# Up and gate projection by seven half-sized products from block 2 on

## The chip, the core and the metric

The kernel runs on one core of one Trainium2 chip. The time is that of the device, in microseconds; before the change it is 2041.45 us, the median of three runs (2039.95 to 2041.57). A core has TensorE (PE) for products, VectorE (DVE), ScalarE (ACT), GpSimd (POOL) and SyncE (SP), which here mostly issues transfers.

## The reference

One layer with modulated layer norms on x of 4 x 1024 x 512: attention with 16 heads over one shared key and value head, then a gated network. The change lies in the network, cut here to what matters:

```python
x = fwht(x * SU_ug) / SCALE
x_up = x @ W_up.T * (Wscale_ug[:INTER] * SCALE)        # 512 -> 2048
x_gate = x @ W_gate.T * (Wscale_ug[INTER:] * SCALE)
x = jax.nn.silu(x_gate) * x_up
x = fwht(x * SU_dp) / SCALE
x = x @ W_down.T * (Wscale_dp * SCALE)                 # 2048 -> 512
```

All arrays are float32. The kernel multiplies them as fp32r, each operand split in a rounded part and a rest, so that one product takes three (rounded by rounded, rounded by rest, rest by rounded).

## The kernel before

After the attention the network runs in 8 blocks (numbered 0 to 7) of 512 tokens. A block has 16 steps (`FT`), numbered f from 0, one for every 128 of the 2048 inner features; g = 16 x block + f counts 128 steps. In step g PE makes up and gate of these 128 features for the block's 512 tokens (`up_gate`: 2 x 4 key tiles x 3 = 24 products of 512 columns), then adds the previous step's share to the four output tiles (`down(g - 1)`: 12 products), so that the other engines have one step to turn up and gate into y.

- SyncE loads the raw weights of step g + 3 (`upgate_raw`, 512 KB, a ring of three) and the down weights of step g + 2 (`d_ring`, 512 KB), both from DRAM, in program order with everything else on its queue.
- ScalarE rounds the raw weights of step g + 1 into `w_ring` (`cast_upgate`), VectorE makes their rest (`split_upgate`).
- When up and gate are done, ScalarE makes silu of the gate, VectorE multiplies it with up and the scale (`weighted`), casts y and makes its rest. `y_mul` counts the product, `y_ready` the split; PE's down products wait for `y_ready`, and `up_gate(g)` for `y_mul` of step g - 2.

Around it each block prepares the next: SyncE loads its rows (`x_in`, `load_block`) in step 1, after the previous block's outputs are stored; VectorE makes the layer-norm statistics in step 2 (`block_statistics`) and the normed rows in step 4; PE transposes them in steps 6 and 7 (`turn`); VectorE combines the four key tiles in steps 8 and 9 (`cross`); in step 10 these are split, and in steps 11 and 12 PE multiplies them with a Hadamard matrix (`had_tile`) into the next block's input `h_t_split`. Step 0 of a block also holds `outputs` of the block before: four output tiles times their gain, and four residual additions, all on VectorE. Block 0 carries the last projection tiles of the attention as well (`TAIL_TILES`).

Every engine works through its own instructions in the order written; semaphores join them. GpSimd does nothing in the network. Nothing plans the order: it is that of the loops and step numbers.

Of the kernel before, what the change touches and what calls it, by code (L numbers as in the profile page):

```python
# [10 lines left out]
P = 128  # L11
D = 512
# [92 lines left out]

def side_work(H, heads):
# [69 lines left out]
def program(nc, io, B, S):  # L176
# [8 lines left out]
    dram = dict(x1=x1_dram, gains=gains_dram, inverse=inverse_dram, qw=qw_dram, across=across_dram, down=down_dram)  # L185
    ctx = ExitStack()
    with ctx:
# [61 lines left out]
        phase(nc, io, dram, B, S, sem, banks, K, A, W, Z, F)  # L249
# [35 lines left out]
def phase(nc, io, dram, B, S, sem, banks, K, A, W, Z, F):  # L285
# [5 lines left out]
    across_rows, down_rows = dram["across"], dram["down"]  # L291
# [14 lines left out]
    ugr, wr, dr, sg, y, ys, gbw, out_sb = (F[n] for n in ("ugr", "wr", "dr", "sg", "y", "ys", "gbw", "out_sb"))  # L306
    up_bank, gate_bank, acc = banks[:, 0:2, :], banks[:, 2:4, :], banks[:, 4:8, :]
# [49 lines left out]

    places = side_places(B)
# [5 lines left out]
    def free_bank(g, k):  # L364

        return banks[:, (g + 1) % 2 + 2 * (k % 2), :]

# [15 lines left out]
    with nc.Block() as block:  # L383

        @block.sync
        def _(sp):
# [93 lines left out]
            def network(g):  # L480
                blk, f = divmod(g, FT)
                if g + UG_RING < STEPS:
                    load_upgate(g + UG_RING)
                if 2 <= g + 2 < STEPS and g:
                    load_down(g + 2)
                if f == X_STEP:
# [120 lines left out]
        def _(act):  # L607
# [89 lines left out]

            def deviations(nb):
# [17 lines left out]
            def network(g):  # L716
                blk, f = divmod(g, FT)
                nb, ahead = blk + 1, blk + 1 < BLOCKS
                if g + 1 < STEPS:
                    cast_upgate(g + 1)  # L720
                act.wait_ge(ug_done, g + 1)
# [4 lines left out]
                if ahead and f == DEV_STEP:  # L726
                    deviations(nb)
                if ahead and f in TURN_STEPS:
                    for k in TURN_STEPS[f]:
                        act.wait_ge(turned, (nb - 1) * KT + k + 1)  # L730
                        turn(nb, k, free_bank(g, k)).then_inc(h2_ready, 1)
                if ahead and f == HI_STEP:
                    round_crossed(nb, range(KT))
                if ahead and f in HAD_STEPS:
                    for k in HAD_STEPS[f]:
# [902 lines left out]
```

## Time and profile before

| | us |
|---|---|
| median of 3 runs | 2041.45 |
| lowest, highest | 2039.95, 2041.57 |
| the profiled execution | 2041.26 |
| its span, first to last instruction | 2039.5 |
| PE busy in it | 1973.9 |
| DVE busy | 1184.8 |
| ACT busy | 794.3 |
| POOL busy | 162.6 |

The busy time of PE counts matmuls whose ends are modelled, so 97% says only that PE is seldom without one. The profile is of one execution; 1.8 us lie around its span.

### The profile page before, as it was taken

What the parts mean: (1) busy time and instruction counts of PE and PEld (TensorE: products, weight loads), DVE (VectorE), ACT (ScalarE), POOL (GpSimd) and SP (SyncE); (2) the same over time, 40 slices, a digit from 0 to 9 for tenths busy, and PEclk for the clock granted to TensorE, in tenths of its full rate; (3) what the DMA queues carried; (4) which work ended last, traced back from release to release, by engine and by line L of the source; (5) the groups of instructions that cost most, each with busy time, mean ns of one, the idle gap of its engine ahead of it and who ended that gap; (6) DMA issues with size and microseconds to landing.
All of it is one profiled execution on the core that took longest, in us unless ns stands there. A gap on an engine that the chain in (4) does not pass through costs nothing.

```text
span 2039.5 us, 26390 instructions
## 1 busy us (share of the span) xinstructions
PE 1973.9 (97%) x9120; PEld 1463.3 (72%) x9120; DVE 1184.8 (58%) x2596; ACT 794.3 (39%) x1333; POOL 162.6 (8%) x530
## 2 busy tenths in 40 slices
PE   6899999999999999999999999999999999999998
PEld 3566666666666556556888888888888888888887
DVE  6777676777667655675455455444554455445433
ACT  3366565556555554465221322222222223232121
POOL 3111121112111111121000000000000000000000
PEclk8899999999999999999999999999999999999999
DMA  7433443334342555635335334344343353443431
GB/s 236 123 98 75 105 114 103 98 84 120 97 115 69 145 160 171 206 118 191 134 134 196 124 127 166 125 132 164 124 165 124 124 171 120 157 141 125 153 125 62
DMA packets 113695, 271.43 MB, mean 133 GB/s; under 512 B 27790, under 2 KB 33166, under 8 KB 113436
## 3 DMA queue, kind: packets, MB, share of 16 engines
q1 hardware_dynamic: 104204, 248.71, 39.9%
q10 hardware_dynamic: 9360, 21.04, 3.1%
q8 instruction: 74, 1.21, 0.3%
q14 instruction: 57, 0.47, 0.1%
HBM read 194.96 MB, written 31.74 MB: 111 GB/s over the span
## 4 chain that ended last, share of the span: by engine, by line
PE 54%; DMA 1%; DVE 1%; POOL 0%; SPq 0%; ACT 0%; issue 0%; POOLq 0%; ACTq 0%; DVEq 0%
PE banks L1311 34%; PE banks L1466 17%; PE banks L1534 1%; PE banks L1402 1%; PE banks L1408 1%; DMA upgate_raw<-in_w_ug 0%; POOL probs L878 0%; PE banks L1511 0%; PE banks L1365 0%; PE banks L1396 0%; DMA inverse_sums_dram<-sums 0%; DVE out_sb L1072 0%; DVE out_sb L1063 0%; DMA o_group<-o_raw 0%; ACT probs L789 0%
## 5 line engine op out<-in xcount | busy, mean ns | idle before, releaser
L1311 PE MATMUL banks<-h_t_split,w_ring 128*128 128x512 f32 x3072 | 717.4, 389 | 1.0 <-DVE w_ring L1037 1.0
L1311 PEld LDWEIGHTS banks<-h_t_split,w_ring 128*128 128x128 f32 x3072 | 576.6, 188 | 121.0 <-DVE w_ring L1037 1.4
L722 ACT ACTIVATE silu_gate<-banks,scale_upgate 128x512 f32<-128x512 f32 x128 | 88.3, 689 | 800.8 <-PE banks L1311 800.8
L1466 PE MATMUL banks<-d_ring,y_split 128*128 128x512 f32 x1536 | 370.5, 390 | 0.1
L1045 DVE SCALAR_TENSOR_TENSOR y<-banks,scale_upgate,silu_gate 128x512 f32<-128x512 f32 x128 | 95.9, 749 | 433.3 <-ACT silu_gate L722 433.3
L789 ACT ACTIVATE probs<-banks 128x512 f32<-128x512 f32 x576 | 312.6, 601 | 60.4 <-PE banks L1511 55.0
L1466 PEld LDWEIGHTS banks<-d_ring,y_split 128*128 128x128 f32 x1536 | 287.3, 188 | 59.5 <-DVE y_split L1051 0.5
L1534 PE MATMUL banks<-probs,v_ones 128*64 128x512 f32 (+3 forms) x1536 | 281.5, 502 | 3.0 <-POOL probs L878 3.0
L1365 PE MATMUL banks<-k_stack,q_stacks 96*128 96x512 f32 (+3 forms) x768 | 252.2, 372 | 16.4 <-ACT neg_max_rows L643 5.7
L1511 PE MATMUL banks<-q_stacks,k_stack 98*128 98x512 f32 (+3 forms) x768 | 251.0, 369 | 6.0 <-ACT probs L789 4.1
L1534 PEld LDWEIGHTS banks<-probs,v_ones 128*64 128x64 f32 x1536 | 119.4, 138 | 164.2 <-issue 136.7
L878 POOL TENSOR_SCALAR_AFFINE_SELECT probs<-probs 128x128 f32<-128x128 f32 x512 | 147.2, 311 | 748.5 <-ACT probs L789 748.5
L1365 PEld LDWEIGHTS banks<-k_stack,q_stacks 96*128 96x128 f32 x768 | 141.7, 192 | 71.8 <-DVE max_all L899 14.9
L899 DVE CUSTOM_DVE_ANT_0 masked_scores<-banks,mask_row,max_all 128x512 f32<-128x512 f32 (+3 forms) x256 | 132.0, 547 | 85.7 <-PE banks L1365 85.1
L1511 PEld LDWEIGHTS banks<-q_stacks,k_stack 98*128 98x128 f32 x768 | 141.3, 191 | 51.5 <-issue 32.7
L902 DVE TENSOR_REDUCE max_all<-banks 128x1 f32<-128x512 f32 x256 | 166.5, 686 | 19.0 <-PE banks L1365 18.7
L1037 DVE TENSOR_TENSOR w_ring<-upgate_raw,w_ring 128x1024 fp32r<-128x1024 f32 x128 | 156.0, 1219 | 17.9 <-ACT w_ring L714 17.6
L767 ACT ACTIVATE o_raw<-banks 128x512 f32<-128x512 f32 x128 | 76.5, 598 | 190.1 <-PE banks L1534 190.1
L899 DVE CUSTOM_DVE_ANT_0 masked_scores<-banks,mask_row 128x512 f32<-128x512 f32 (+3 forms) x256 | 120.0, 486 | 40.1 <-PE banks L1365 38.8
L714 ACT ACTIVATE w_ring<-upgate_raw 128x1024 fp32r<-128x1024 f32 x128 | 135.0, 1055 | 9.5 <-DMA upgate_raw<-in_w_ug 9.5
L1311 PE MATMUL banks<-h_t_split,qw_group 128*128 128x512 f32 x384 | 94.5, 402 | 2.9 <-DVE h_t_split L929 2.5
L1311 PE MATMUL banks<-ow_split,o_split 128*128 128x512 f32 x384 | 93.3, 392 | 2.6 <-DVE q_split L920 2.6
(132 smaller groups left out, 1247.6 us busy)
## 6 DMA issues: line engine op xcount, KB each, us to landing
upgate_raw<-in_w_ug SPq DMA_DIRECT2D x128, 512.0 KB, 4.2
d_ring<-down_split_dram SPq DMA_DIRECT2D x128, 512.0 KB, 3.3
q_stacks<-q_split SPq DMA_DIRECT2D x192, 128.0 KB, 2.5
o_group<-o_raw SPq DMA_DIRECT2D x128, 128.0 KB, 2.3
x<-in_x SPq DMA_DIRECT2D x32, 256.0 KB, 3.0
o_group<-inverse_sums_dram SPq DMA_DIRECT2D x64, 128.0 KB, 2.7
x_and_residual<-in_x SPq DMA_DIRECT2D x32, 256.0 KB, 4.4
x_dram<-x_and_residual SPq DMA_DIRECT2D x32, 256.0 KB, 2.5
```

Source lines behind the costliest of these rows:

```text
L714: nc.scalar.activation(wr[g % 2][:, 0], ugr[g % UG_RING][:], ACT.Copy).then_inc(ug_cast, 1)
L789: nc.scalar.activation(pr[:, u, :], score_bank[:, at % SLOTS_SCORE, :], ACT.Exp, scale=SCALE).then_inc(exped, 1)
L878: last = nc.gpsimd.affine_select(out=triangle, in_=triangle, compare_op=ALU.is_ge, fill=0.0, base=0, pattern=[[1, P]], channel_multiplier=-1)
L899: last = nc.vector.tensor_tensor_reduce(out=masked_scores[:, i % 2, col:col + w], in0=part, in1=mask[:, HALF - w:HALF], scale=1.0, scalar= ...
L902: last = nc.vector.tensor_reduce(out, part, AX.X, ALU.max)
L1037: nc.vector.tensor_tensor(wr[g % 2][:, 1], ugr[g % UG_RING][:], wr[g % 2][:, 0].bitcast(F32), ALU.subtract).then_inc(ug_ready, 1)
L1045: nc.vector.scalar_tensor_tensor(out=y[:], in0=up_bank[:, s, :], scalar=sug[:, 0, f:f + 1], in1=sg[:, s, :], op0=ALU.mult, op1=ALU.mult).t ...
L1311: ins = nc.tensor.matmul(out, weights(a, k), moving(m, k), start=(k == 0 and a + m == 0), stop=(last and k == kts - 1 and a == 1))
L1365: last = nc.tensor.matmul(side[:, r, col:col + w], qst[0:96, s, qt * P:(qt + 1) * P], kst[0:96, b % 2, k0:k0 + w], start=True, stop=True)
L1466: last = nc.tensor.matmul(acc[:, t, :], ys[s][:, a, t * P:(t + 1) * P], dr[g % D_RING][:, m, :], start=(f == 0 and a + m == 0), stop=(f == ...
L1511: last = nc.tensor.matmul(score_bank[:, at % SLOTS_SCORE, col:col + w], kst[0:98, b % 2, kt * P:(kt + 1) * P], qst[0:98, s, q0:q0 + w], st ...
L1534: last = nc.tensor.matmul(obank[half * 2 * HD:(half + 1) * 2 * HD, c, q0 - c * HALF:q0 - c * HALF + w], vs[:, b % 2, kt, :], pr[:, u, col: ...
```

## The change

From block 2 on (`PLAIN = 2`, `FIRST_HALVES = 32`) up and gate are taken as one product of a 2 x 2 block matrix: rows up and gate (128 features each), columns the first and the second 256 keys, times an input of two halves of keys by two halves of 256 tokens (`TOKENS`). Strassen's scheme, in Winograd's form, makes it of seven half-sized products (`ITEMS`) in place of eight: 7 x 2 key tiles x 3 = 42 products of 256 columns.

- Weight items. Three of the seven are weights as they are, four are sums. In block 1 GpSimd makes the sums (`sum_weights`), one set in each step, from the raw weights that lie in `upgate_raw` anyhow; ScalarE rounds them and VectorE or GpSimd makes their rests; ScalarE issues the store of the split set (1792 KB) to `upgate_items_dram`. In blocks 2 to 7 SyncE loads one such set in each step, three steps ahead, into a ring of three (`load_items`); raw weights are no longer loaded, cast and split there.
- Input items. Four of the seven inputs are sums too: GpSimd makes them once a block from a copy of the Hadamard tiles (`sum_inputs`), ScalarE rounds all seven and VectorE makes the rests, in steps 13 to 15.
- Outputs. VectorE adds the seven results up into gate and up (`add_both`, `add_gates`, `add_ups`, `multiply_second`), in halves of 256 tokens. The last of the seven (`UP_LAST`) is multiplied after `down(g - 1)`. ScalarE rounds y now.
- The residual additions move from step 0 to step 1 of a block (from block 2 on).

The diff, cut to its core:

```diff
@@ SyncE
             def load_upgate(g):
                 if g >= UG_RING:
                     sp.wait_ge(ug_ready, g - UG_RING + 1)
+                if g - UG_RING >= FIRST_HALVES - FT:
+                    sp.wait_ge(items_lo, g - UG_RING - (FIRST_HALVES - FT) + 1)
+                    sp.wait_ge(weights_summed, 3 * (g - UG_RING - (FIRST_HALVES - FT) + 1))
                 sp.dma_start(ugr[g % UG_RING][:], io["w_ug"][g % FT]).then_inc(ug_in[g % UG_RING], 16)
+            def load_items(n):
+                if n == 0:
+                    sp.wait_ge(items_out[0], 16 * FT // 2)
+                if n == 1:
+                    sp.wait_ge(items_out[1], 16 * FT // 2)
+                    sp.wait_ge(ug_done, FIRST_HALVES)
+                if n >= HALVES_RING:
+                    sp.wait_ge(products_made, ITEMS * (n - HALVES_RING + 1))
+                r = (n + 2) % HALVES_RING
+                sp.dma_start(wq[r][:].bitcast(F32), items_dram[n % FT]).then_inc(items_in[r], 16)
@@ ScalarE
             def network(g):
+                f, made = g % FT, g - (FIRST_HALVES - FT)
+                if g + 1 < FIRST_HALVES:
                     cast_upgate(g + 1)
+                if made >= 0:
+                    store_items(made)
+                if -1 <= made < FT - 1:
+                    round_items(made + 1)
+                    round_sums(made + 1)
                 act.wait_ge(ug_done, g + 1)
@@ GpSimd
+            def sum_weights(f):
...
+                nc.gpsimd.tensor_tensor(s1, a21, a22, ALU.add).then_inc(weights_summed, 1)
+                nc.gpsimd.tensor_tensor(s3, a11, a21, ALU.subtract)
+                pool.wait_ge(weights_summed, 3 * f + 1)
+                nc.gpsimd.tensor_tensor(s2, s1, a11, ALU.subtract).then_inc(weights_summed, 1)
+                pool.wait_ge(weights_summed, 3 * f + 2)
+                nc.gpsimd.tensor_tensor(s4, a12, s2, ALU.subtract).then_inc(weights_summed, 1)
+                pool.wait_ge(sums_hi, f + 1)
+                nc.gpsimd.tensor_tensor(cw[f % 2][:, 1, 3:ITEMS, :], sraw[:], cw[f % 2][:, 0, 3:ITEMS, :].bitcast(F32), ALU.subtract).then_inc(sums_lo, 1)
@@ VectorE
+            def halves(g):
+                blk, f = divmod(g, FT)
+                if g > FIRST_HALVES:
+                    multiply_second(g - 1)
+                add_both(g)
+                if g > FIRST_HALVES:
+                    split_half(g - 1, 1)
+                add_gates(g)
+                add_ups(g)
+                multiply_first(g)
+                split_half(g, 0)
+                if f == 0:
+                    outputs(blk - 1)
+                if f == 1:
+                    for t in range(NT):
+                        residual(blk - 1, t)
+                if blk + 1 < BLOCKS:
+                    around(g)
@@ TensorE
+            def half_product(g, item):
+                blk, r = g // FT, (g - FIRST_HALVES + 2) % HALVES_RING
+                for k in range(2):
+                    for a, m in ((0, 0), (0, 1), (1, 0)):
+                        last = nc.tensor.matmul(item_bank(g, item), wq[r][:, a, item, k * P:(k + 1) * P], by_key(item_input(blk, item, m))[:, k, :],
+                                                start=(k == a + m == 0), stop=(k == a == 1))
+                last.then_inc(products_made, 1)
...
+            for g in range(FIRST_HALVES, STEPS):
+                half_products(g)
+                for i in range(2):
+                    beside_halves(g, i)
+                    down(g - 1, i * NT // 2, (i + 1) * NT // 2)
+                beside_read(g)
+                last_half_product(g)
             down(STEPS - 1)
```

On VectorE, a plain step of the network before, of 128 features by 512 tokens:

```order
L1037 TENSOR_TENSOR w_ring<-upgate_raw,w_ring 128x1024
L1045 SCALAR_TENSOR_TENSOR y<-banks,scale_upgate,silu_gate 128x512
L1050 CAST y_split<-y 128x512
L1051 TENSOR_TENSOR y_split<-y,y_split 128x512
```

And the same step in block 1 of the changed kernel, where `items_made` and `items_ring` take the weight items:

```order
L1244 TENSOR_TENSOR w_ring<-upgate_raw,w_ring 128x1024
L1273 TENSOR_TENSOR items_made<-upgate_raw,items_made 128x512
L1274 TENSOR_TENSOR items_made<-upgate_raw,items_made 128x256
L1252 SCALAR_TENSOR_TENSOR y<-banks,scale_upgate,silu_gate 128x512
L1257 CAST y_split<-y 128x512
L1258 TENSOR_TENSOR y_split<-y,y_split 128x512
```

Two subtractions stand ahead of the product y. GpSimd, idle before in the network, has these five beside them in the same step (the set after each other one goes to `items_ring`):

```order
L1062 TENSOR_TENSOR weight_sums<-upgate_raw 128x256
L1063 TENSOR_TENSOR weight_sums<-upgate_raw 128x256
L1065 TENSOR_TENSOR weight_sums<-weight_sums,upgate_raw 128x256
L1067 TENSOR_TENSOR weight_sums<-upgate_raw,weight_sums 128x256
L1069 TENSOR_TENSOR items_made<-weight_sums,items_made 128x1024
```

On VectorE again, steps 1 and 2 of a later block of the changed kernel, with what each waits for:

```order
L1304 SCALAR_TENSOR_TENSOR y<-y,scale_upgate,silu_gate 128x256 [waits silu_ready,halves_added]
L1324 TENSOR_TENSOR y_split<-y,y_split 128x256 [waits halves_hi]
L1385 TENSOR_TENSOR out_sb<-out_sb,x_in 128x512 [waits acc_read] x4
L1317 TENSOR_TENSOR y<-y,banks 128x256 [waits halves_added,products_made]
L1304 SCALAR_TENSOR_TENSOR y<-y,scale_upgate,silu_gate 128x256 [waits dve_step]
L1281 TENSOR_TENSOR both<-banks,up_first 128x256 [waits p1_copied,products_made]
L1324 TENSOR_TENSOR y_split<-y,y_split 128x256 [waits halves_hi]
L1288 TENSOR_TENSOR all_gate<-banks,both 128x256 [waits halves_added,products_made]
L1290 TENSOR_TENSOR silu_gate<-banks,all_gate 128x512 [waits y_mul,dve_step]
L1297 TENSOR_TENSOR y<-banks,both 128x256 [waits y_ready]
L1299 TENSOR_TENSOR y<-banks,up_first 128x256 [waits products_made]
```

The residual additions (L1385) now stand at the end of step 1, behind its second split; before, they stood in step 0 right behind the outputs. On SyncE's queue the place of the block load before and after:

```order
L463 DMA upgate_raw<-in_w_ug 128x1024 [waits ug_ready]
L472 DMA d_ring<-down_split_dram 128x1024 [waits d_done]
L478 DMA out<-out_sb 128x512 [waits out_ready] x4
L458 DMA x_in<-x_dram 128x4x512 [waits out_ready]
```

```order
L556 DMA d_ring<-down_split_dram 128x1024 [waits d_done]
L547 DMA items_ring<-upgate_items_dram 128x3584 [waits products_made]
L562 DMA out<-out_sb 128x512 [waits out_ready] x4
L528 DMA x_in<-x_dram 128x4x512 [waits out_ready]
```

The stores and the block load have kept their place in the queue, and what stands ahead of them is an items load of 3584 elements a partition, released by the last product of step 1, where there was one of 1024.

## Rows read from the trace of the kernel before

**Rows 1.** The page, parts 1, 2 and 5: engines, clock by slices, costliest groups.
```profile
PE 1973.9 (97%) x9120; PEld 1463.3 (72%) x9120; DVE 1184.8 (58%) x2596; ACT 794.3 (39%) x1333; POOL 162.6 (8%) x530
...
PEclk8899999999999999999999999999999999999999
...
L1311 PEld LDWEIGHTS banks<-h_t_split,w_ring 128*128 128x128 f32 x3072 | 576.6, 188 | 121.0 <-DVE w_ring L1037 1.4
```

**Rows 2.** The page, part 4: the chain that ended last, shares by line.
```profile
PE banks L1311 34%; PE banks L1466 17%; PE banks L1534 1%; PE banks L1402 1%; PE banks L1408 1%; DMA upgate_raw<-in_w_ug 0%; POOL probs L878 0%; PE banks L1511 0%; PE banks L1365 0%; PE banks L1396 0%; DMA inverse_sums_dram<-sums 0%; DVE out_sb L1072 0%; DVE out_sb L1063 0%; DMA o_group<-o_raw 0%; ACT probs L789 0%
```

**Rows 3.** Busy time by window: one step, and its columns.
```profile
core 0: us, PE busy (x) PEld busy (x) DVE busy (x) ACT busy (x) POOL busy (x), PEclk, DMA share, GB/s
1500.00:1508.16 8.16, 8.16 (x37) 6.76 (x37) 4.56 (x8) 1.64 (x2) 0.00 (x0) 1.00 0.40 124
```

**Rows 4.** The chain in order of time: start us, us, what. Two block starts.
```profile
1597.91 5.45 PE banks L1311 x24
...
1732.14 5.45 PE banks L1311 x24
```

**Rows 5.** Timeline of PE in the attention: start us, us, instructions.
```profile
801.23 0.40 PE L1511 MATMUL banks<-q_stacks,k_stack 98*128 98x256 f32 x2
801.47 2.92 PE L1311 MATMUL banks<-ow_split,o_split 128*128 128x512 f32 x12
```

**Rows 6.** Timelines of GpSimd and VectorE at the start of the program.
```profile
22.99 1.26 POOL L866 TENSOR_TENSOR qw_group<-x_and_residual,qw_group 128x512 fp32r<-128x512 f32 x1 [9.92 <-ACT qw_group L831]
23.01 1.79 DVE L929 TENSOR_TENSOR h_t_split<-kv,h_t_split 128x512 fp32r<-128x512 f32 x1
24.21 1.72 POOL L868 TENSOR_TENSOR kvw_split<-masked_scores,kvw_split 128x512 fp32r<-128x512 f32 x1
...
36.01 1.34 DVE L935 CAST k_stack<-kv 96x512 fp32r<-96x512 f32 x1 [1.78 <-ACT kv L626]
37.39 1.66 DVE L936 TENSOR_TENSOR k_stack<-kv,k_stack 32x512 fp32r<-32x512 f32 x1
```

**Rows 7.** Groups by line, shapes apart: busy us, mean ns | idle before.
```profile
L1037 DVE TENSOR_TENSOR w_ring<-upgate_raw,w_ring 128x1024 fp32r<-128x1024 f32 x128 | 156.0, 1219 | 17.9 <-ACT w_ring L714 17.6
L714 ACT ACTIVATE w_ring<-upgate_raw 128x1024 fp32r<-128x1024 f32 x128 | 135.0, 1055 | 9.5 <-DMA upgate_raw<-in_w_ug 9.5
L1045 DVE SCALAR_TENSOR_TENSOR y<-banks,scale_upgate,silu_gate 128x512 f32<-128x512 f32 x128 | 95.9, 749 | 433.3 <-ACT silu_gate L722 433.3
L1051 DVE TENSOR_TENSOR y_split<-y,y_split 128x512 fp32r<-128x512 f32 x128 | 88.6, 692 | 4.4
L1050 DVE CAST y_split<-y 128x512 fp32r<-128x512 f32 x128 | 54.6, 427 | 4.4
L899 DVE CUSTOM_DVE_ANT_0 masked_scores<-banks,mask_row 128x256 f32<-128x256 f32 x64 | 26.9, 420 | 0.0
L630 ACT ACTIVATE v_ones<-banks 128x256 f32<-128x256 f32 x4 | 1.5, 372 | 0.0
```

**Rows 8.** Timeline of VectorE and SyncE's queue around a block load; its landing.
```profile
1507.78 2.49 DVE L1072 TENSOR_TENSOR out_sb<-out_sb,x_in 128x512 f32<-128x512 f32 x4
1508.49 2.14 SPq L478 DMA_DIRECT2D out<-out_sb  x4
...
1510.67 0.46 SPq L458 DMA_DIRECT2D x_in<-x_dram  x1
...
DMA to landing us min/median/max: 5.9/5.9/5.9
...
1521.71 2.46 DVE L995 BATCH_NORM_STATS2 ln_stats<-x_in 128x6 f32<-128x512 f32 x4
1524.21 0.38 DVE L999 BATCH_NORM_AGGREGATE ln_mean_var<-ln_stats 128x2 f32<-128x6 f32 x4
```

**Rows 9.** Busy time by window: the queue when it is full (columns as above).
```profile
1509.00:1519.00 10.00, 10.00 (x46) 8.29 (x45) 5.41 (x8) 1.64 (x2) 0.00 (x0) 1.00 0.98 351
1514.00:1518.00 4.00, 4.00 (x20) 3.30 (x19) 0.76 (x1) 0.00 (x0) 0.00 (x0) 1.00 1.04 417
```

More of the change, by code:

```diff
@@ new lines, in around, with round_half @@
+            def around(g):
+                blk, f = divmod(g, FT)
+                nb, ahead = blk + 1, blk + 1 < BLOCKS
+                if ahead and f == DEV_STEP:
+                    deviations(nb)
+                if ahead and f == HI_STEP:
+                    round_crossed(nb, range(KT))
+                if ahead and nb >= PLAIN and f in INPUT_STEPS:
+                    round_inputs(nb, INPUT_STEPS[f])
+            def round_half(g, half):
+                n, at = g - FIRST_HALVES, slice(half * TOKENS, (half + 1) * TOKENS)
+                if half:
+                    act.wait_ge(y_mul, g + 1)
+                else:
+                    act.wait_ge(halves_added, ADDED * n + FIRST_MULTIPLIED)
+                    act.wait_ge(d_done, g - 1)
+                nc.scalar.activation(ys[g % 2][:, 0, at], y[:, at], ACT.Copy).then_inc(halves_hi, 1)
@@ L725, in network @@
                         round_group(ALL // 4 - 2 + g // 2, half)
[L726 to L735, printed above, removed]
-                        act.wait_ge(had_done, (nb - 1) * KT + k + 1)
-                        round_had(nb, k, free_bank(g, k))
+                for i in range(2):
+                    read_tile(g, i)
+                around(g)
             def side_step(keys):
@@ L1051, in weighted, with rest_of_inputs @@
                 nc.vector.tensor_tensor(ys[s][:, 1, :], y[:], ys[s][:, 0, :].bitcast(F32), ALU.subtract).then_inc(y_ready, 1)
+            def rest_of_inputs(nb, f):
+                m = nb - PLAIN
+                done = sum(len(INPUT_STEPS[step]) for step in INPUT_STEPS if step < f)
+                for i, item in enumerate(INPUT_STEPS[f]):
+                    dve.wait_ge(inputs_hi, ITEMS * m + done + i + 1)
+                    nc.vector.tensor_tensor(by_key(item_input(nb, item, 1)), input_half(item), by_key(item_input(nb, item, 0)).bitcast(F32),
+                                            ALU.subtract).then_inc(inputs_lo, 1)
@@ new lines, in around @@
+            def around(g):
+                blk, f = divmod(g, FT)
+                nb = blk + 1
+                if f == STATS_STEP:
+                    for t in range(NT):
+                        block_statistics(nb, t)
+                if f == NORM_STEP:
+                    block_inverses(nb)
+                    for t in range(NT):
+                        block_rows(nb, t)
+                if f in (CROSS_STEP, CROSS_STEP + 1):
+                    cross(nb, f - CROSS_STEP)
+                if f == HI_STEP:
+                    for ks in ((0, 1), (2, 3)):
+                        crossed_rest(nb, ks)
+                if nb >= PLAIN and f in INPUT_STEPS:
+                    rest_of_inputs(nb, f)
@@ L1587, in _ @@
             weigh(ALL - 1, 1)
-            for g in range(STEPS):
+            for g in range(FIRST_HALVES):
                 up_gate(g)
```

291 lines of the change are left out of this document (253 added, 38 removed).

## The prediction

> **What bounds the kernel now.** I read the page's busy shares and clock first: TensorE is busy 97% of 2039.5 us, at full granted clock in every slice but the first two [rows 1]. The chain of what ended last says the same by line: 34% products of up and gate, 17% down products, nearly nothing else in the last 800 us [rows 2]. One step of the network is 8.16 us, in which PE never rests while VectorE works 4.56 and ScalarE 1.64 [rows 3]. Of it 24 products of 512 columns take 5.44 us (5.45 in [rows 4]), or 0.2267 each, and the 12 down products the other 2.72. A whole block of 16 steps is 134.2 us (two block starts, 134.23 apart [rows 4]): 130.6 for 16 steps and 3.7 for the transposes and Hadamard tiles. So PE's own work is the price of a block, and anything that makes PE wait is added in full.
>
> **What is removed: columns.** From block 2 on (blocks are numbered 0 to 7), 96 steps issue 42 products of 256 columns instead of 24 of 512: 10752 columns for 12288. The trace has no such row on a 128-row weight, so I bound it. Half of 0.2267 is 0.1133. Two score products of 256 columns, each with its own weights, take 0.24 us from start to next start, 0.12 each [rows 5]. I take 0.117, nearer the row than the rule of three. 42 x 0.117 = 4.91 us against 5.44, 0.53 a step, 96 steps: **-50.5 us** (-65 with 0.1133, -38 with 0.12). A step is then 7.64 us. The recorded 188 ns of a weight load [rows 1] is no spacing: in [rows 5] two loads and two products fit in 0.24 us.
>
> **What is added in block 1: a port that two engines share.** In steps 15 to 31 GpSimd now makes the weight sums: per step four adds of 256 columns and one subtraction of 1024. A subtraction of 512 columns took it 1.26 us [rows 6], so I take, by size, 4 x 0.65 + 2.6 = 5.2 us. VectorE gets two more subtractions (512 and 256 columns). Alone, GpSimd's 5.2 and the 1.05 us in which it waits for ScalarE to round the sums fit in 8.16 us. But [rows 6] show that the two engines exclude each other: a VectorE subtraction from SBUF, 0.69 us for its like [rows 7], took 1.79 beside GpSimd's, and ended 0.55 after it; GpSimd's next took 1.72; a VectorE cast took 1.34 for 0.43 and the subtraction behind it 1.66 for 0.68. The SBUF — State Buffer page of the Trainium skill (Who interferes with whom) has this rule: VectorE with two SBUF inputs, or in a two-port mode, takes a port pair that it shares with GpSimd, and the later one waits for the whole instruction; one PSUM input does not contend. By that rule, and the trace agrees with 1.79 against 0.69, both lists below must be added up; without it this block would cost nothing.
> VectorE's list per step, durations from [rows 7]: the ring split 1.22, the new 0.69 and 0.42, the cast of y 0.43, its rest 0.69, together 3.45. With GpSimd's 5.2 that is 8.65 us a step for one pair, 138.4 in 16 steps. Around them in that block come the rows of the norm (four, at the cast's 0.43) 1.7, the four crossings of 1024 columns 4.9, their rest 2.4, residuals 2.5 [rows 8], seven input remainders 4.8, and GpSimd's four input sums 5.0: 21.3. Together 159.7 us for a block of 134.2. The delay reaches PE because ScalarE's silu stands behind its rounding of the sums, SyncE's next raw load behind both, and the stored items must be back before step 32: **+26 us**. From both sides: 0 if the pair is not the limit, +35 if it also idles half a microsecond a step while GpSimd waits for ScalarE.
>
> **What is moved: the residual, and with it the load of the next block.** Before, outputs and residuals both run in step 0 of a block; the load is issued at 1510.67, right behind them, lands 5.9 us later, and the statistics start only at 1521.71, 5 us after the landing [rows 8]. After, the residuals stand in step 1 behind the second split. Take T2, the start of step 2. SyncE's items load for a later step, 1.835 MB where a raw load was 0.524, is released by step 1's last product and issued at T2 + 0.5. Each residual ends 0.62 after the one before, the last at T2 + 2.4; four stores and the block load are out by T2 + 3.2. That is 1.84 + 1.05 + 1.05 = 3.93 MB in one queue, at 417 GB/s [rows 9] 9.4 us from T2 + 1.4; landing T2 + 11.5. VectorE wants it at T2 + 7.7. It waits, spends 2.9 on the statistics [rows 8], then 0.43 + 0.48 to finish y, and 0.43 on the first sum of step 3, which PE needs before its sixth item: ready at about T2 + 16. PE is there at 5 x 0.70 = 3.5 us into step 3, which began at T2 + 7.7: some 4.7 us of wait. Four blocks give 19, block 2 (its queue still full of items that were stored late) about 7.8: **+26.5 us**. The last block loads nothing. The wait shrinks by 1 us for each microsecond that the load lands earlier, to nothing at T2 + 7.
>
> **Smaller terms.** The last input remainders: VectorE ends its own step at 7.2 and then has two more of 0.69, so the next block starts at 8.5, not 7.64: 0.9 in five blocks and 2 at step 32, **+6.5**. The Hadamard steps wait for ScalarE's copy between two tiles: 0.6 in five blocks, **+3**. At the end the second half of y is added, multiplied, rounded and split only after the last product, 0.43 + 0.48 + 0.37 + 0.43 and the hops, 2.1 us of which 0.5 was waited for before: **+1.6**.
>
> **What lies hidden.** The VectorE work of a steady step: seven of 256 columns (0.42 each, the row of the scores' own 256), two scaled products at 0.48, one of 512, 4.6 us; its chain from the fifth item (3.5 + 0.2) is 0.42 + 0.69 + 0.42 + 0.42 + 0.48, ScalarE's 0.37, and 0.42, done at 7.2 of 7.64 us with hops. So the cover is only 0.45 us; each 0.1 us beyond it would cost 10 us. The transfers: 2.36 MB a step, 309 GB/s, where one queue held 351 over 10 us with gaps and 417 without [rows 9]. In block 1, 1.84 out and 1.05 in make 354 GB/s, near that; it fits, barely.
>
> **Sum.** -50.5 + 26 + 26.5 + 6.5 + 3 + 1.6 = +13. The profiled execution took 2041.26 us (span 2039.5 and 1.8 around it), 0.2 under the median of 2041.45, so the forecast is 2055 us.
>
> **Rivals.** (A) The forecast, 0.46; its own range is 2045 to 2070.
> (B) The shared pair costs little, because GpSimd has half a step of lead and VectorE's idle 3.6 us a step [rows 3] take it up. Then -13: 2029, faster. For it: the sum is 6% over what a step has. Against: the 21.3 us around, and each wait is for a whole instruction. It decides if block 1 takes under 147 us. 0.19.
> (C) The block load is not late, because the queue's transfers interleave: -13.5, 2028. Against: x_in took 5.9 us with only the end of the stores ahead [rows 8]. 0.07.
> (D) Narrow products cost 0.1133 or less: 2055 - 15 = 2040, same or a bit faster; 0.12.
> (E) VectorE's chain is over 7.64 us and sets every step: at +0.25 us, +24, 2079. For it: nine hops between engines, of 0.05 to 0.1 us. 0.13.
> (F) Weight loads or transfers set the step: if a load really occupied 188 ns, 42 of them would be 7.9 us and the kernel some 300 us slower; if items came at 300 GB/s the step would be 7.87, +22. 0.03.
>
> The measurement tells 0.2% (4 us) from no change. Faster: B, C and half of D, 0.31; same 0.06; slower 0.63. The range 2020 to 2084 takes in B and C with the low product price, and E.
>
> **What would show it.** Starts of the first item in successive steps 7.6 to 7.7 us apart in blocks 2 to 7; items of six products 0.70 us. Block 1 over 150 us, GpSimd busy most of it, and subtractions of VectorE there longer than 1.22 and 0.69. In step 2 or 3 of a block VectorE idle for 3 to 4 us before the statistics on the block load, and a PE wait of 4 to 5 us. The prediction is wrong if block 1 is near 134 us (B), if the statistics find their data (C), or if steady steps exceed 7.8 us (E).

## The result, and the profile after the change

The changed kernel takes 2074.68 us (median of 4 runs, 2070.3 to 2075.89) against 2041.03 for the kernel before (4 runs, 2039.95 to 2041.57): a ratio of 1.0162, 95% interval 1.0144 to 1.0179. It is slower, as forecast, by 33.6 us where the sum said 13. That is inside the stated range of 2020 to 2084 us, which was wide, and above the 2045 to 2070 that the prediction gave its own account (rival A). The profiled execution spans 2071.7 us, 32.2 more than that of before, and the decomposition below is made against that.

The page of the changed kernel, parts 1, 2 and 5, answers to [rows 1]: TensorE is now idle for a part of the span, and its clock dips in one slice after the start.

```profile
PE 1957.6 (94%) x10848; PEld 1524.7 (74%) x10848; DVE 1393.8 (67%) x3222; ACT 869.8 (42%) x1615; POOL 304.0 (15%) x634
...
PEclk8899999999999999999999998999999999999999
...
L1742 PE MATMUL banks<-h_t_split,items_ring 128*128 128x256 f32 x2304 | 329.6, 286 | 43.9 <-DVE both L1281 36.4
```

In its chain (part 4, answering to [rows 2]) the products of up and gate (L1742 and L1620) and of down (L1828) have 43% of the span where they had 51%, and the block load, which was not in it, has 3%:

```profile
PE banks L1742 21%; PE banks L1828 14%; PE banks L1620 8%; DMA x_in<-x_dram 3%; DVE out_sb L1385 1%; PE banks L1897 1%; PE banks L1711 1%; PE banks L1717 1%; DVE ln_stats L1202 1%; DMA upgate_items_dram<-items_made 1%; ACT silu_gate L865 0%; DMA items_ring<-upgate_items_dram 0%; DVE silu_gate L1290 0%; DMA upgate_raw<-in_w_ug 0%; DVE out_sb L1376 0%
```

**A plain step.** Timeline of PE in block 2 (start us, us, instructions; the first six of a row of 12 on `h_t_split` are the last item of the step before, whose place is behind the down products):

```profile
1356.93 1.59 PE L1742 MATMUL banks<-h_t_split,items_ring 128*128 128x256 f32 x12
1358.36 1.60 PE L1742 MATMUL banks<-input_sums,items_ring 128*128 128x256 f32 x12
1359.80 0.88 PE L1742 MATMUL banks<-h_t_split,items_ring 128*128 128x256 f32 x6
1360.52 0.88 PE L1742 MATMUL banks<-input_sums,items_ring 128*128 128x256 f32 x6
1361.24 0.88 PE L1742 MATMUL banks<-h_t_split,items_ring 128*128 128x256 f32 x6
1361.96 2.91 PE L1828 MATMUL banks<-d_ring,y_split 128*128 128x512 f32 x12
1364.71 1.48 PE L1742 MATMUL banks<-h_t_split,items_ring 128*128 128x256 f32 x11
```

From 1356.93 to 1361.96 are 42 products in 5.03 us, 0.1198 each; the down products take 2.75, and the next step follows 7.78 us after this one. Before it was 8.16. So 96 steps give back 0.38 each: -36.5 us. The down products are the same 12 as before, when they took 2.72.

**Step 3 of a block.** The start times of the steps, read from PE's timeline for every block, are 7.78 us apart with two kinds of exception that were there before (turn and Hadamard steps), and one that was not: step 3. It takes 18.9 us in block 2 and 16.5, 17.2, 18.3 and 16.0 in blocks 3 to 6. In block 3 step 2 starts at 1397.31 (T2) and step 3 at 1405.09. Here are SyncE's queue, the landing of that block load, then VectorE and PE, answering to [rows 8]:

```profile
1397.51 0.32 SPq L547 DMA_DIRECT2D items_ring<-upgate_items_dram  x1
1397.87 2.16 SPq L562 DMA_DIRECT2D out<-out_sb  x4
1400.14 0.38 SPq L528 DMA_DIRECT2D x_in<-x_dram  x1
```

```profile
DMA to landing us min/median/max: 11.6/11.6/11.6
```

```profile
1404.09 0.43 DVE L1324 TENSOR_TENSOR y_split<-y,y_split 128x256 fp32r<-128x256 f32 x1 [0.48 <-ACT y_split L850]
1411.79 2.48 DVE L1202 BATCH_NORM_STATS2 ln_stats<-x_in 128x6 f32<-128x512 f32 x4 [7.27 <-DMA x_in<-x_dram]
1414.30 0.38 DVE L1206 BATCH_NORM_AGGREGATE ln_mean_var<-ln_stats 128x2 f32<-128x6 f32 x4
1414.59 0.39 DVE L1317 TENSOR_TENSOR y<-y,banks 128x256 f32<-128x256 f32 x1
1415.01 0.48 DVE L1304 SCALAR_TENSOR_TENSOR y<-y,scale_upgate,silu_gate 128x256 f32<-128x256 f32 x1
1415.41 0.42 DVE L1281 TENSOR_TENSOR both<-banks,up_first 128x256 f32<-128x256 f32 x1
```

```profile
1407.97 0.88 PE L1742 MATMUL banks<-input_sums,items_ring 128*128 128x256 f32 x6
1415.89 1.65 PE L1742 MATMUL banks<-h_t_split,items_ring 128*128 128x256 f32 x6 [7.04 <-DVE both L1281]
1417.33 3.69 PE L1828 MATMUL banks<-d_ring,y_split 128*128 128x512 f32 x12
```

VectorE has nothing to do from 1404.52 until the block is there at 1411.76, and `both` (L1281), on which PE's sixth item waits, stands behind the statistics in its program. PE idles 7.04 us. When it starts again it is slow: six products take 1.65 us where 0.88 was, twelve down products 3.69 where 2.91 was. The windows (columns as in [rows 3]) show why:

```profile
1400.00:1404.00 4.00, 4.00 (x26) 3.59 (x26) 3.01 (x7) 1.50 (x3) 0.00 (x0) 1.00 1.00 315
1404.00:1408.00 4.00, 4.00 (x34) 3.92 (x33) 0.43 (x1) 0.44 (x2) 0.00 (x0) 1.00 0.95 365
1408.00:1412.00 4.00, 0.85 (x8) 0.65 (x6) 0.21 (x1) 0.00 (x0) 0.00 (x0) 1.00 1.09 441
1412.00:1416.00 4.00, 0.11 (x1) 0.11 (x1) 3.79 (x12) 0.45 (x2) 0.00 (x0) 0.52 0.97 410
1416.00:1420.00 4.00, 4.00 (x15) 3.47 (x16) 2.39 (x6) 3.56 (x4) 0.00 (x0) 0.63 0.18 73
```

PE stops at 1408.85. The window that ends at 1412 still has the full clock, the next, idle to its end, has 0.52 (near the lower of its two levels, 1.2 GHz), and PE's first 4 us of work have 0.63 on average. The slow products are 0.77 and 0.78 us on top of the wait. Excess of step 3: 8.7 = 7.04 + 0.77 + 0.78 + 0.1. Over the five blocks it is 11.1 + 8.7 + 9.4 + 10.5 + 8.2 = **47.9 us**: 36.4 of waits (6.5 to 8.1 each), the rest nearly all slow products behind them.

**Block 1.** It takes 142.9 us (1092.99 to 1235.84) against 134.23 before: +8.6. (The two lines of [rows 4] are starts of step 12 of blocks 4 and 5, not of blocks; their distance is a block's all the same.) In it GpSimd and VectorE run beside each other, for example:

```profile
1131.96 2.66 POOL L1069 TENSOR_TENSOR items_made<-weight_sums,items_made 128x1024 fp32r<-128x1024 f32 x1 [1.74 <-ACT items_made L810]
...
1139.61 2.53 POOL L1069 TENSOR_TENSOR items_ring<-weight_sums,items_ring 128x1024 fp32r<-128x1024 f32 x1 [1.39 <-ACT items_ring L810]
```

```profile
1131.15 1.22 DVE L1244 TENSOR_TENSOR w_ring<-upgate_raw,w_ring 128x1024 fp32r<-128x1024 f32 x1
1132.28 2.88 DVE L1273 TENSOR_TENSOR items_made<-upgate_raw,items_made 128x512 fp32r<-128x512 f32 x1
```

A subtraction of 512 columns takes 2.88 us beside GpSimd's of 1024, where its like took 0.69 [rows 7]. But the ring split ahead of it, with two SBUF inputs as well, takes its 1.22 us as before: it starts in the 1.74 us in which GpSimd waits for ScalarE. From one large GpSimd subtraction to the next are 7.65 us here, less than a step. Over the 16 sets this distance is 7.2 to 8.7 us in nine cases and 9.8 to 14.8 in six, 9.07 on average.

Most steps of the block keep their 8.16 us. Steps 1 and 2, 2.0 and 1.7 us longer, show how the rest comes about (VectorE, then PE):

```profile
1104.38 5.24 DVE L1385 TENSOR_TENSOR out_sb<-out_sb,x_in 128x512 f32<-128x512 f32 x4
```

```profile
1111.34 7.31 PE L1620 MATMUL banks<-h_t_split,w_ring 128*128 128x512 f32 x24 [1.87 <-DVE w_ring L1244]
```

The four residual additions take 5.24 us beside GpSimd where 2.49 was [rows 8]. The ring split behind them is late, PE waits 1.87 us for it, and the 24 products behind that wait take 7.31 where 5.60 was; the granted clock is 0.60 from 1112 to 1116.

**Start of block 2.** Its first step takes 11.7 us and its second 9.35: PE waits for the second set of items, which SyncE may load only once the sets of block 1 are stored (its queue waits 7.8 us for that store and issues the load at 1239.71). Timeline of PE; the second step's 1.6 us over are slow products behind the wait:

```profile
1235.84 0.98 PE L1742 MATMUL banks<-h_t_split,items_ring 128*128 128x256 f32 x6 [1.31 <-DVE h_t_split L1265]
...
1247.52 1.04 PE L1742 MATMUL banks<-h_t_split,items_ring 128*128 128x256 f32 x6 [3.64 <-DMA items_ring<-upgate_items_dram]
1248.36 2.76 PE L1742 MATMUL banks<-input_sums,items_ring 128*128 128x256 f32 x12
```

**The end.** Before, the last 24 down products took 6.02 us without a break; now half of them wait for the second half of y, and after the wait the clock is low again (PE timeline, and the window of the last products):

```profile
2062.74 4.42 PE L1828 MATMUL banks<-d_ring,y_split 128*128 128x512 f32 x12 [1.94 <-DVE y_split L1324]
```

```profile
2064.00:2068.00 4.00, 3.16 (x8) 1.93 (x6) 3.90 (x7) 0.00 (x0) 0.00 (x0) 0.57 0.32 119
```

The parts make up the whole: 1.4 less ahead of block 1, +8.6 in it, -36.5 for the steps, +47.9 in step 3, +5.4 at the start of block 2 (its first two steps, 11.68 and 9.35), +3.9 for the input remainders (step 15 takes 8.46, five times), +2.5 for the turn steps (each pair adds 2.3 where it added 1.8), +3.2 up to the last product and 1.3 less behind it. That is +32.3; measured 32.2.

### The profile page after: what moved, and what is told of

Read it like the earlier page. It is cut to its first block, busy times and chain, and to the rows that moved or that the text cites. A ratio compares the mean times of both kernels' runs of the same rounds, so it can differ in the third digit from the quotient of the medians.

```text
span 2071.7 us, 31351 instructions
## 1 busy us (share of the span) xinstructions
PE 1957.6 (94%) x10848; PEld 1524.7 (74%) x10848; DVE 1393.8 (67%) x3222; ACT 869.8 (42%) x1615; POOL 304.0 (15%) x634
## 4 chain that ended last, share of the span: by engine, by line
PE 45%; DMA 4%; DVE 4%; ACT 1%; issue 1%; POOL 1%; SPq 1%; DVEq 0%; ACTq 0%; POOLq 0%
PE banks L1742 21%; PE banks L1828 14%; PE banks L1620 8%; DMA x_in<-x_dram 3%; DVE out_sb L1385 1%; PE banks L1897 1%; PE banks L1711 1%; PE banks L1717 1%; DVE ln_stats L1202 1%; DMA upgate_items_dram<-items_made 1%; ACT silu_gate L865 0%; DMA items_ring<-upgate_items_dram 0%; DVE silu_gate L1290 0%; DMA upgate_raw<-in_w_ug 0%; DVE out_sb L1376 0%
## 5 line engine op out<-in xcount | busy, mean ns | idle before, releaser
L1828 PE MATMUL banks<-d_ring,y_split 128*128 128x512 f32 x1536 | 386.1, 399 | 2.0 <-DVE y_split L1324 1.9
L1742 PE MATMUL banks<-h_t_split,items_ring 128*128 128x256 f32 x2304 | 329.6, 286 | 43.9 <-DVE both L1281 36.4
L1742 PEld LDWEIGHTS banks<-h_t_split,items_ring 128*128 128x128 f32 x2304 | 305.6, 193 | 57.4 <-DVE both L1281 37.4
L1828 PEld LDWEIGHTS banks<-d_ring,y_split 128*128 128x128 f32 x1536 | 288.1, 193 | 59.5 <-DVE y_split L1324 2.1
L1742 PE MATMUL banks<-input_sums,items_ring 128*128 128x256 f32 x1728 | 239.8, 284 | 0.0
L1742 PEld LDWEIGHTS banks<-input_sums,items_ring 128*128 128x128 f32 x1728 | 222.3, 193 | 0.0
L1620 PE MATMUL banks<-h_t_split,w_ring 128*128 128x512 f32 x768 | 181.6, 393 | 4.7 <-DVE w_ring L1244 4.0
L1109 DVE TENSOR_REDUCE max_all<-banks 128x1 f32<-128x512 f32 x256 | 166.4, 685 | 18.9 <-PE banks L1674 18.6
L1874 PEld LDWEIGHTS banks<-q_stacks,k_stack 98*128 98x128 f32 x768 | 141.3, 191 | 51.1 <-issue 32.3
L1620 PEld LDWEIGHTS banks<-h_t_split,w_ring 128*128 128x128 f32 x768 | 144.8, 189 | 37.0 <-DVE w_ring L1244 5.6
L850 ACT ACTIVATE y_split<-y 128x256 fp32r<-128x256 f32 x192 | 79.8, 416 | 158.8 <-DVE y L1304 158.8
L865 ACT ACTIVATE silu_gate<-silu_gate,scale_upgate 128x512 f32<-128x512 f32 x96 | 69.2, 721 | 165.4 <-DVE silu_gate L1290 165.3
```

Of the source, the lines that this page charges most:

```text
L850: nc.scalar.activation(ys[g % 2][:, 0, at], y[:, at], ACT.Copy).then_inc(halves_hi, 1)
L1109: last = nc.vector.tensor_reduce(out, part, AX.X, ALU.max)
L1620: ins = nc.tensor.matmul(out, weights(a, k), moving(m, k), start=(k == 0 and a + m == 0), stop=(last and k == kts - 1 and a == 1))
L1742: last = nc.tensor.matmul(item_bank(g, item), wq[r][:, a, item, k * P:(k + 1) * P], by_key(item_input(blk, item, m))[:, k, :], start=(k == ...
L1828: last = nc.tensor.matmul(acc[:, t, :], ys[s][:, a, t * P:(t + 1) * P], dr[g % D_RING][:, m, :], start=(f == 0 and a + m == 0), stop=(f == ...
L1874: last = nc.tensor.matmul(score_bank[:, at % SLOTS_SCORE, col:col + w], kst[0:98, b % 2, kt * P:(kt + 1) * P], qst[0:98, s, q0:q0 + w], st ...
```

## The experiments

Two theories at first, by the letters of the expectations. **M**: the block load is late because the residuals moved to step 1, as the heading of that term in the prediction says. **Q**: it is late because of what stands in the queue ahead of it (an items load of 1792 KB, released by step 1's last product), and VectorE asks for it in step 2; the residual has nothing to do with it.

**1. Statistics one step later.** The three steps of the norm move by one.

```diff
-X_STEP, STATS_STEP, DEV_STEP, NORM_STEP, CROSS_STEP, HI_STEP = 1, 2, 3, 4, 8, 10
+X_STEP, STATS_STEP, DEV_STEP, NORM_STEP, CROSS_STEP, HI_STEP = 1, 3, 4, 5, 8, 10
```

> One edit to the changed kernel: statistics, deviations and normed rows of the next block one step later (3, 4, 5 in place of 2, 3, 4); the block load stays where it is. Theory Q (the block load lands late, VectorE stands at the statistics and PE behind it): in the changed kernel the load lands 15.2 us after the start of step 2, and VectorE would now come to it at about 15.5, so the waits of 8.3 to 11 us in five blocks (48 us together) go: 2074.7 - 48 = 2027 us, under the kernel before. Rival R (the wait is VectorE's and ScalarE's own work around the statistics, the square root and its table loads): the wait only moves one step on, 2060 to 2075 us.

Measured: 2027.73 us (5 runs), ratio to before 0.994 (0.9928 to 0.9953). One constant turns a loss of 33 us into a gain of 13. The block load still takes 10.4 to 12.3 us, and nobody waits for it; step 3 takes 7.78 in every block and step 4, into which a wait could have moved, at most 7.85. VectorE at the end of its list for step 3 of block 3; PE's step 4 starts at 1403.65:

```profile
1402.99 2.46 DVE L1202 BATCH_NORM_STATS2 ln_stats<-x_in 128x6 f32<-128x512 f32 x4
1405.49 0.38 DVE L1206 BATCH_NORM_AGGREGATE ln_mean_var<-ln_stats 128x2 f32<-128x6 f32 x4
```

The statistics start without idle time ahead of them, and `both` of step 4 is done at 1407.02, when PE has yet to start its fifth item (1407.25). So their 2.9 us are hidden where the data are there. Rival R, by which the wait would only move on, falls. The span falls by 46.0; from the start of block 2 on it is 47.9, the sum read from step 3 (the rest lies ahead, where the edit changes little). So the wait and what hangs on it are that term.

**2. Residuals back in step 0**, as before the change.

```diff
-                if f == 1:
-                    for t in range(NT):
-                        residual(blk - 1, t)
...
-                if blk < PLAIN - 1:
+                if blk < BLOCKS - 1:
```

> One part of the change undone: the residual additions stand again in step 0 of a block, behind the outputs; SyncE's queue is as in the changed kernel. Theory M (what the prediction headed that part with: the load is late because the residuals moved): the load goes out a step earlier, 30 to 48 us gained less some 15 for VectorE's fuller step 0, 2045 to 2060 us. Theory Q (it is late because it stands behind an items load that is released only by step 1's last product): the load goes out where it did, nothing is gained there, and VectorE's 2.5 us more in step 0 make PE wait some 2.8 us in step 1 of six blocks: 2074.7 + 15 = 2090 us.

Measured: 2084.24 us (4 runs), ratio 1.0214 (1.02 to 1.0228). M falls: the kernel is 10 us slower still. PE in block 3, and the block load, whose residuals are done 8 us before its issue:

```profile
1395.36 0.98 PE L1739 MATMUL banks<-h_t_split,items_ring 128*128 128x256 f32 x6 [1.71 <-DVE both L1281]
...
1418.03 1.65 PE L1739 MATMUL banks<-h_t_split,items_ring 128*128 128x256 f32 x6 [6.86 <-DVE both L1281]
```

```profile
1391.64 2.49 DVE L1382 TENSOR_TENSOR out_sb<-out_sb,x_in 128x512 f32<-128x512 f32 x4
...
1402.39 0.38 SPq L528 DMA_DIRECT2D x_in<-x_dram  x1
```

It is issued behind the same items load as before (T2 + 2.8 again, T2 being 1399.64), which waits for the last product of step 1; and outputs and residuals together in step 0 make `both` of step 1 late, so that this step is 1.96 us longer in blocks 3, 5, 6 and 7 and 2.3 in block 4. So with this order in the queue the new place of the residuals saves about 2 us a block and delays nothing; experiment 4 has the other order.

**3. Stores and block load ahead of the items load** in step 1.

```diff
-                if FIRST_HALVES <= g + HALVES_RING < STEPS:
-                    load_items(g + HALVES_RING - FIRST_HALVES)
                 if f == X_STEP:
                     if blk:
                         store_block(blk - 1)
                     if blk + 1 < BLOCKS:
                         load_block(blk + 1)
+                if FIRST_HALVES <= g + HALVES_RING < STEPS:
+                    load_items(g + HALVES_RING - FIRST_HALVES)
```

> One edit to the changed kernel: in step 1 of a block SyncE issues the stores and the block load ahead of the items load, not behind it. Theory Q: 1.8 MB fewer ahead in the queue and the load lands some 6 us earlier, at about 9.5 us after the start of step 2; the wait of 8.3 to 11 us falls to 2 to 4: 2074.7 - 30 = 2045 us. Theory M: no gain, since the residuals still stand in step 1, 2070 to 2078 us.

Measured: 2035.76 us (10 runs), ratio 0.9972 (0.9963 to 0.9981). The load lands 6.1 us after its issue, about as before the change (5.9 in [rows 8]); VectorE waits 5.7 us for it in blocks 3 to 6 together and PE 4.8. Landing of the block loads, and PE's waits (us in total, times, longest), from 1300 us on:

```profile
DMA to landing us min/median/max: 6.0/6.1/6.5
```

```profile
PE banks L1742 <- DVE both L1281: 4.8, 4, 2.1
```

Step 3 is down to 8.9 to 10.1 us in blocks 3 to 6, and 14.2 in block 2.

**4. Edits 2 and 3 together.**

> Both edits: residuals in step 0, stores and block load ahead of the items load. Theory Q: the load goes out about 7 us into step 1 and lands before VectorE wants it; the 48 us of waits go, the 15 of VectorE's fuller step 0 come: 2042 us. If M alone were right this would equal the run with the residuals moved back.

Measured: 2040.74 us (10 runs), ratio 1.0004 (0.9995 to 1.0014). Step 3 is 7.78 in blocks 3 to 6, so here the residuals do let the load start earlier, once the items load is out of its way; but step 1 takes 9.74 (11.67 in block 4, slow products behind the wait), and the pair is 5 us worse than edit 3 alone.

**5. GpSimd's weight sums narrow.** From the third set on its four sums and its subtraction take 8 columns a group where 256 were, so that most columns of the stored sums are not made; everything else (ScalarE's rounding, VectorE's remainders, stores and loads) stays. On top of edit 1. The question is whether the shared port, or the sets and their transfers themselves, cost what is left in block 1 and at the start of block 2.

```diff
...
+                w, v = (P, 2 * P) if f < 2 else (4, 8)
-                a11, a12, a21, a22 = (ugr[g % UG_RING][:, k:k + 2, n, :] for n in range(2) for k in (0, 2))
+                a11, a12, a21, a22 = (ugr[g % UG_RING][:, k:k + 2, n, 0:w] for n in range(2) for k in (0, 2))
...
```

> The kernel of the run with the later statistics (2027.7 us), and in it GpSimd's weight sums and their rests cut to the first 8 of 256 or 1024 columns from the third set on, so most columns of the stored sums are stale; transfers, rounding, the number of instructions and their order stay. Its block 1 took 143.5 us where the kernel before has 134.2, and PE waits 3.7 us more for items at the start of block 2. Theory P (GpSimd's long instructions on the port it shares with VectorE, and the sets they finish late): block 1 comes back to 134 to 136 us and the wait at the start of block 2 shrinks, 2027.7 - 9 - 3 = 2015 us. Rival X (it is the transfers, 1.8 MB out and 1 MB in per step): block 1 stays at 142 to 144 us, 2027 us.

Measured: 2013.85 us (4 runs), ratio 0.9869 (0.9855 to 0.9882). Block 1 is 135.7 us, where edit 1 alone had 143.5, and block 2 129.8 where it had 134.8. VectorE's remainders of 512 columns in block 1, those of each other set, changed kernel first, then this one (groups by line: us, mean ns; the sets between them go from 1458 to 850 ns):

```profile
L1273 DVE TENSOR_TENSOR items_made<-upgate_raw,items_made 128x512 fp32r<-128x512 f32 x8 | 17.5, 2191 | 0.0
```

```profile
L1274 DVE TENSOR_TENSOR items_made<-upgate_raw,items_made 128x512 fp32r<-128x512 f32 x8 | 6.1, 766 | 0.0
```

The wide GpSimd work costs 12.8 us: 7.8 in block 1 and 5.0 in block 2, whose first two steps fall back to 7.88 and 7.78. The span is 14.6 shorter, but 2.2 of it stand ahead of block 1, where both kernels do the same work (block 1 starts between 1091.9 and 1094.5 us in all profiles of before, the changed kernel and experiments 1 to 7), and 0.4 are lost again in block 5. The same transfers run in both, so they are not the cause. The edit takes away GpSimd's own time together with its hold on VectorE, and does not tell the two apart: that VectorE is held shows in its rows, that a free but slow GpSimd would deliver the sets in time is not shown.

**6. Items in DRAM as two rows of 7168 bytes a partition** in place of one of 14336, on the changed kernel: is the items load slow for its row size?

```diff
-    items_dram = nc.dram_tensor("upgate_items_dram", (FT, P, 2, ITEMS, 2 * P), F32).ap()
+    items_dram = nc.dram_tensor("upgate_items_dram", (FT, 2, P, ITEMS, 2 * P), F32).ap()
...
```

> The changed kernel with the items in DRAM laid so that a row of a partition is 7168 bytes twice, not 14336 once; same bytes, same order. An items load now takes 7.0 us from issue to landing where 1.835 MB at 417 GB/s and 1.8 us around it would be 6.2, and packets of 14336 bytes at its start take 1.2 us where later ones take 0.54. Theory D (the size of the packets holds up the transfer's start, and the block load behind it): items land in 6.3 us or less, the block load 1 us earlier, 2074.7 - 5 = 2070 us. Rival N (the slow start is the transfer's own, whatever its rows): 2073 to 2076 us and the same landing.

Measured: 2076.36 us (4 runs), ratio to before 1.018 (1.0163 to 1.0197), no different from the changed kernel's (2070.3 to 2075.89; here 2075.04 to 2080.63). Landing of the items loads from 1240 to 2000 us, two rows first, then one:

```profile
DMA to landing us min/median/max: 6.9/7.3/15.4
```

```profile
DMA to landing us min/median/max: 6.8/7.2/14.7
```

**7. Edits 1 and 3 together.**

> Both edits that take the block load's wait away: statistics one step later, and stores and block load ahead of the items load. In the run with the later statistics no wait of steps 2 to 5 was left in blocks 3 to 7, so little more is to be had: 2024 to 2029 us, if the theory that the block load's landing was the whole of it holds; more than 5 us better would mean that its lateness costs elsewhere too.

Measured: 2027.05 us (5 runs), ratio 0.9933 (0.9921 to 0.9946). Nothing on top of edit 1: with the wait gone the order in the queue is worth nothing.

**8. The price of a narrow product by itself**: in the kernel before, each run of 24 products of 512 columns becomes 48 of 256, the same columns in all.

```diff
-                    last = product(bank[:, s, :], lambda a, k: wr[s][:, a, k, n, :], lambda m, k: fht[blk % 2][:, m, k, :], KT)
+                    for h in range(2):
+                        at = slice(h * HALF // 2, (h + 1) * HALF // 2)
+                        last = product(bank[:, s, at], lambda a, k: wr[s][:, a, k, n, :], lambda m, k: fht[blk % 2][:, m, k, at], KT)
```

> The kernel before, its 24 up and gate products of 512 columns in a step issued as 48 of 256, nothing else changed: the price of a narrow product by itself. Theory F (a fixed part of 13 ns a product, 0.1197 us as in the changed kernel): 48 x 0.1197 = 5.75 us for 5.44, 128 steps, 2041 + 39 = 2080 us. The value of the prediction, 0.117: 2041 + 22 = 2063. Proportional price, 0.1133: 2041.

Measured: 2083.08 us (1 run, span 2081.3, 41.8 above that of before). PE, one step:

```profile
1500.36 5.92 PE L1311 MATMUL banks<-h_t_split,w_ring 128*128 128x256 f32 x48
1506.11 2.91 PE L1468 MATMUL banks<-d_ring,y_split 128*128 128x512 f32 x12
```

48 products in 5.75 us, 0.1198 each, as in the changed kernel, and the down products behind them take 2.75 where 2.72 was, as there. By these rows two products of 256 columns cost 12.9 ns more than one of 512 (0.2396 less 0.2267); the span, with the down products and the rest in it, grows by 41.8 us for 3072 more products, 13.6 ns for each. Here VectorE has less to do than in the changed kernel and no items are loaded, so neither sets the 7.78 us step: the product itself costs that.

## Why the prediction was right in sign and wrong in size

**What bounds the kernel** held: PE's waits are added in full, and each term above was found as idle or slow time of PE.

**The removed columns** (-50.5): -36.5. I chose 0.117 between 0.1133 and 0.12, "nearer the row than the rule of three". The row, two products of the scores, was right as it stood: 0.1198 measured. With 0.12 the prediction's own bound of -38 would have stood. 14 us of the error are this term: 11.3 are the 0.117 (42 products, 96 steps), 2.9 the down products, which the sum left at 2.72. Put another way, a product has a fixed part of 12.9 ns, for 18 more products in each of 96 steps 22.3 us; 0.117 holds 7.3 ns of it, 12.6 us. The page "TensorE: Matmul & The Clock Gate" of the Trainium skill (Back-to-back issue gap) gives 262 cycles for 256 columns and 518 for 512, 109 and 216 ns at 2.4 GHz; the traces have 119.8 and 226.7, so both are some 11 ns over it.

**The shared port** (+26 in block 1): +7.3 there (the 8.6 without the 1.3 of the input remainders, below), and with the 5.4 at the start of block 2 12.7 in all; experiment 5, on the kernel of experiment 1, gives back 7.8 and 5.0. That the engines hold each other up was right (2.88 us for 0.69); the step that failed is "both lists below must be added up". Added up, with the 21.3 us around them, they are 159.7 us, 9.98 for a set, and 8.65 without; that holds only if neither engine's waits overlap with the other's work. In the trace a set takes 9.07 on average and in nine of 15 cases 7.2 to 8.7, since pieces of VectorE's list fall into the 1.2 to 2.7 us in which GpSimd waits for ScalarE. And PE feels it only where VectorE has more than the pair: in steps 1 and 2 behind the residuals, in 14 and 15 behind the input remainders (waits of 1.55 and 1.31 us), and in step 11, whose 0.69 us have no releaser in the profile. Of the 8.6, 1.7 are slow products. Rival B named this reason, "VectorE's idle 3.6 us a step take it up", and its bound, block 1 under 147 us, was met; it did not cost nothing, as B had it.

**The block load** (+26.5): +47.9. This term had the right place, the right waiting instruction and the right queue, and three of its numbers were close: in block 3 the load was issued at T2 + 2.8 (predicted 3.2), VectorE was ready for it at T2 + 7.2 (7.7), and `both` was done 4.1 us after the landing (4.5). Two failed. First the landing: T2 + 14.4, not 11.5 (and the prediction's own figures, 9.4 us from T2 + 1.4, give 10.8). I divided 3.93 MB by the 417 GB/s of a 4 us window of the kernel before; its 351 over 10 us [rows 9] would have given 11.2 us. The trace of the changed kernel splits the stretch. The items load's 128 packets (14336 bytes each) run from 1398.45 to 1405.80, and until 1404.5 hardly anything else moves; then come the 1024 packets of stores and block load (2048 bytes each), the last ending at 1411.22. Windows of these two parts, all engines (columns as in [rows 3]):

```profile
1398.40:1404.50 6.10, 6.10 (x43) 5.61 (x42) 4.99 (x12) 1.77 (x4) 0.00 (x0) 1.00 1.00 294
1404.50:1411.74 7.24, 4.35 (x37) 4.15 (x35) 0.02 (x1) 0.38 (x1) 0.00 (x0) 1.00 1.05 409
```

So the items load by itself moved at 294 GB/s, though the engines show as busy throughout, and took 6.1 us where 417 makes 4.4. Behind it the rate was 409, but some 0.8 of the 3.0 MB begun then were packets of the down load and the next items load, both issued behind the block load (their first packets start at 1409.38 and 1410.64); at that rate they take about 2 us, which is the rest. Why the items load starts slowly is open; experiment 6 shows that its row size is not the reason. Second, the clock, which the term did not have: in block 3 the wait of 7 us costs another 1.55 through slow products behind it, and over the five blocks 36.4 us of waits became 47.9. Together 2.3 us of wait and 1.6 of clock make the 4.7 into 8.7. The title of the term, "the residual, and with it the load of the next block", was wrong as a cause: experiments 2 and 3 put it on the items load ahead in the queue, and experiment 1 on the step in which the statistics ask. Undoing the move by itself made the kernel slower.

**Smaller terms.** Input remainders: 6.5 predicted, 3.9 in steps 15 and 0, and the 2 us at step 32 were there as 1.3 (the wait for `h_t_split`): 5.2. The Hadamard steps' +3 did not come: a pair adds 1.84 us, before 1.86; the turn steps took 2.5 instead, which I had not priced. The end: 1.6 predicted, 3.2 up to the last product and 1.3 less behind it, 1.9.

**What lay hidden** stayed so: in plain steps PE has no wait for VectorE, whose chain fits (rival E falls), and items loads land in 7.2 us, three steps ahead of their use. Rival C falls, and rival D had the price on the wrong side.

So the +13 of the sum became +32.3: +14.0 for the product price, +21.4 for the block load, -13.3 for the port, -3 and +2.5 for Hadamard and turn steps, -1.3 for the input remainders, +0.3 for the end and -1.4 ahead of block 1, where nothing was changed. That the forecast missed by 19 us only is luck: the port's error hid more than half of the block load's, and with the port at its measured 12.7 and the rest as predicted, the sum would have been nothing (13 less 13.3).

## What to carry to other kernels

When a load in a shared queue grows from 0.5 to 1.8 MB, look at what is issued behind it and at which instruction, in an in-order engine, asks for that first. Moving that consumer one step later was worth 47 us (experiment 1), reordering the queue 39 (experiment 3). Replacing few wide products by many narrow ones pays only after the fixed part of each: count products as well as columns. And where two engines exclude each other, lay their work out along the step with its waits; adding up the lists gave twice what it cost here.

Of the kernels that make all their sums, that of experiment 1 (with that of experiment 7 beside it) is the fastest, 13.2 us (0.65%) faster than the kernel before. What is left to gain in it are at most the 12.8 us of block 1's sums, which could be spread over the two blocks in which raw weights are loaded; that was not tried.

## What the runs showed of the hardware that I had not expected

- The clock after a wait: twelve products of 256 columns took 2.76 us for 1.60 behind a wait of 3.64 us, twelve down products 3.69 for 2.91 a little after one of 7.04, with 0.52 and 0.63 granted, and 4.42 at the end, behind one of 1.94 (0.57 granted). Behind the 1.71 us wait of experiment 2 there is nothing of it (2.91). In block 1 of the changed kernel a wait of 1.87 us had it (7.31 for 5.60) and one of 1.55 did not (5.73). The same last wait of 1.94 us was followed by twelve products at full speed in experiment 3 and slow ones in experiment 1 (timelines of PE, in that order), and so was a wait of 3.6 us at the start of block 2: that step takes 7.87 us in experiment 3 and 9.35 in the changed kernel. Why is not settled here.

```profile
2024.65 3.01 PE L1828 MATMUL banks<-d_ring,y_split 128*128 128x512 f32 x12 [1.94 <-DVE y_split L1324]
```

```profile
2016.77 4.52 PE L1828 MATMUL banks<-d_ring,y_split 128*128 128x512 f32 x12 [1.94 <-DVE y_split L1324]
```

- A product takes 0.1198 us for 256 columns and 0.2267 for 512, so two narrow ones cost 12.9 ns more than a wide one; by the span it is 13.6 (41.8 us for 3072 more of them).
- This the prediction had, but not how unequal it is. Beside GpSimd's subtraction of 1024 columns a VectorE subtraction with two SBUF inputs waits for its end (2.88 us for 0.69) and so do casts (683 ns for 427 on average in block 1), while the product y, with an input in PSUM, keeps 742 ns. The Trainium skill has this on its page "SBUF — State Buffer" (Who interferes with whom), and the trace agrees.
